# Attention scores in fp16 parts and packed banks: one change to a four-branch kernel on one Trainium2 core

## What is computed

```python
q, k = rope(q), rope(k)            # 32 query heads, 8 key heads, width 16
scores = einsum("bhqd,bhkd->bhqk", q, k) / 4
masked = where(causal, scores, NEG)
chunk_max = masked.reshape(b, 32, s, s // 16, 16).max(-1)
top = top_k(chunk_max, 8)          # 8 chunks of 16 keys for each query
allowed = causal & (in_top | (k_pos < 128) | (k_pos > q_pos - 128))
attn = softmax(where(allowed, scores, NEG))
out = attn @ v
```

## Time and profile before

| | |
|---|---|
| median of three runs | 1491.49 us |
| the profiled execution | 1492.17 us, of which the traced span is 1490.4 us |
| busy in the span: PE / DVE / ACT / POOL | 1314.6 / 1047.9 / 870.6 / 452.0 us |
| `project` | 472.8 to 602.9 us from the span's start |
| `attention` | 602.9 to about 1345 us |
| granted clock, mean | 0.938 |

### The profile page before, as it was taken

How to read it: one execution, slowest core, us unless ns; L and a number is a source line. 1 busy time by engine, 2 the same in 40 slices (tenths; PEclk the granted TensorE clock), 3 DMA queues, 4 the chain that set the end, 5 groups by cost and what they waited for, 6 DMA issues and landing times. The chain is left out here.

```text
span 1490.4 us, 35636 instructions
## 1 busy us (share of the span) xinstructions
PE 1314.6 (88%) x10686; PEld 697.9 (47%) x10686; DVE 1047.9 (70%) x3535; ACT 870.6 (58%) x1605; POOL 452.0 (30%) x1388
## 2 busy tenths in 40 slices
PE   8957999999996995799899898998989989986996
PEld 3423444444443553355455454554545545543663
DVE  5875656566553697688788787887878878852563
ACT  2525626354241564477678676776768767772553
POOL 3430000000002332344343343433433434431665
PEclk9976999999998997699999999999999999998997
DMA  9310000000000366301111011110111100002221
GB/s 339 144 42 1 1 1 0 0 0 0 0 1 4 102 161 160 129 5 36 41 39 39 7 36 41 39 39 7 39 37 39 39 13 33 10 9 57 57 78 43
DMA packets 65132, 69.74 MB, mean 47 GB/s; under 512 B 35214, under 2 KB 53774, under 8 KB 64300
## 3 DMA queue, kind: packets, MB, share of 16 engines
q1 hardware_dynamic: 64940, 67.38, 14.0%
HBM read 36.96 MB, written 19.92 MB: 38 GB/s over the span
## 5 line engine op out<-in xcount | busy, mean ns | idle before, releaser
L1362 DVE TENSOR_REDUCE arena<-bank 128x32 f32<-128x512 f32 (+3 forms) x768 | 395.7, 549 | 108.6 <-PE bank L1209 53.7
L1300 ACT ACTIVATE arena<-bank 128x512 f32<-128x512 f32 x576 | 336.2, 611 | 178.2 <-PE bank L1220 103.7
L1206 PE MATMUL bank<-arena 96*128 96x512 bf16 (+3 forms) x768 | 248.6, 348 | 27.8 <-issue 20.5
L1220 PE MATMUL bank<-arena 123*128 123x512 bf16 x576 | 225.4, 397 | 8.9 <-ACT arena L1300 6.9
L1239 PE MATMUL bank<-arena 128*32 128x128 f32 x4608 | 171.0, 276 | 12.2 <-ACT arena L1300 12.2
L579 PE MATMUL bank<-arena 128*128 128x512 f16 (+1 forms) x704 | 171.0, 386 | 0.0
L1458 POOL TENSOR_SCALAR arena<-arena 128x128 bf16<-128x128 bf16 x384 | 143.9, 375 | 43.8 <-DVE arena L1408 19.7
L1446 POOL TENSOR_TENSOR arena<-arena 128x4 f32<-128x4 f32 x128 | 25.6, 200 | 379.8 <-DVEq L1380 379.8
L1239 PEld LDWEIGHTS bank<-arena 128*32 128x32 f32 x4608 | 119.5, 109 | 43.0 <-ACT arena L1300 24.7
L1206 PEld LDWEIGHTS bank<-arena 96*128 96x128 bf16 x768 | 72.1, 100 | 119.2 <-DVE arena L1362 54.5
L205 POOL TENSOR_TENSOR arena<-arena 128x1 f32<-128x1 f32 x32 | 7.6, 236 | 383.3 <-DVE arena L201 382.9
(11 more groups left out here) (182 smaller groups left out, 2257.4 us busy)
## 6 DMA issues: line engine op xcount, KB each, us to landing
arena<-qk_rows SPq DMA_DIRECT2D x16, 960.0 KB, 4.8
qk_rows<-arena SPq DMA_DIRECT2D x16, 768.0 KB, 4.1
arena<-arena SPq DMA_DIRECT2D x32, 256.0 KB, 2.6
arena<-in_x SPq DMA_DIRECT2D x4, 1024.0 KB, 12.3
out<-arena SPq DMA_DIRECT2D x16, 256.0 KB, 2.1
qk_rows<-arena SPq DMA_DIRECT2D x16, 192.0 KB, 4.6
arena<-in_down_qT SPq DMA_DIRECT2D x1, 2816.0 KB, 25.6
arena<-in_up_qT SPq DMA_DIRECT2D x1, 2752.0 KB, 18.1
```

The source lines that it names most:

```text
L1206: last = pe.matmul(bank[:, 0:k1 - k0], query_aug[st.slot][0:ROWS, h * P:(h + 1) * P], key_aug[st.p][0:ROWS, k0:k1], start=True, stop=not d ...
L1220: last = pe.matmul(bank[:, :], key_aug[st.p][0:KROWS, j * P:(j + 1) * P], query_aug[st.slot][0:KROWS, f * N:(f + 1) * N], start=True, stop ...
L1300: act.activation(probs[u % PROBS], back_bank[u % 2][:, :], ACT.Exp, scale=float(HD) ** -0.5).then_inc(probs_ready, 1)
L1362: dve.tensor_reduce(out=cm[:, h * 64 + k0 // CHUNK:h * 64 + k1 // CHUNK], in_=score_bank[bank_of_score(front, number)][:, 0:k1 - k0].rearr ...
```

## The change

q and k are split into two fp16 parts instead of three bf16 parts: three part products, 48 rows instead of 96. The mask rows move from PSUM and operand row 96 to row 64, the rows between (48 to 63) being zeroed once. Minus the maximum is one fp16 row instead of three bf16 ones. All mask rows of a head (49) are in one set, so each head's mask is turned once and `keep_q` copies once. Score banks are filled to 512 columns, with a head ending and the next beginning inside a bank: a step has `i + 1` banks instead of 4 or 8. For `i < 2` only the maximum of each head is taken. `schedule` assumes 0.65 us for each bank.

The diff, cut to its core ("..." where lines are left out):

```diff
-ROWS = 6 * HD
+TERMS = 3
+ROWS = TERMS * HD
+MASK_AT = 64
-MASK_ROWS = 3 * CPT + PARTS
-KROWS = ROWS + MASK_ROWS
+MASK_ROWS = (SEQ_TILES - 2) * CPT + 1
+KROWS = MASK_AT + MASK_ROWS
...
     # project, ScalarE and VectorE
-                act.activation(slots(q_rows[b])[:, :, 0:3, :], q_of(part[b][0], 3), ACT.Copy)...
+                act.activation(slots(q_rows[b])[:, :, 0:2, :], q_of(part[b][0], 2), ACT.Copy)...
-                    dve_seq.mark(dve.tensor_tensor(out=rotated[b], in0=rotated[b], in1=high, op=ALU.subtract))
-                    dve_seq.wait(dve)
-                    dve_seq.mark(dve.tensor_copy(mid, rotated[b]))
-                    dve_seq.wait(dve)
-                    dve_seq.mark(dve.tensor_tensor(out=low, in0=rotated[b], in1=mid, op=ALU.subtract))
+                    dve_seq.mark(dve.tensor_tensor(out=low, in0=rotated[b], in1=high, op=ALU.subtract))
...
-                    dve_seq.mark(dve.tensor_copy(kk[:, :, 0:4:3, :], k_of(high, 2)))
-                    dve_seq.mark(dve.tensor_copy(kk[:, :, 5:6, :], k_of(high, 1)))
-                    dve.tensor_copy(kk[:, :, 1:5:3, :], k_of(mid, 2))
-                    dve.tensor_copy(q[:, :, 3:5, :], q_of(mid, 2))
+                    dve.tensor_copy(kk[:, :, 0:3:2, :], k_of(high, 2))
...
+                dve.memset(m.key_aug[k][32:MASK_AT, :], 0.0)
...
     # attention, TensorE
+            pe.wait_ge(query_blank, 1)
-                    last = pe.transpose(turn_bf[0:ROWS, ...], staged[st.p][:, at:at + ROWS], m.ident_bf)
+                    last = pe.matmul(turn_bank[0:ROWS, ...], staged[st.p][:, at:at + ROWS], m.ident_half, ...)
-                    for f in range(1 + st.two):
-                        last = pe.transpose(turn_bf[ROWS:KROWS, ...], w[:, h, f, 0:MASK_ROWS], m.ident_bf)
+                    last = pe.matmul(turn_bank[MASK_AT:KROWS, ...], w[:, h, 0:MASK_ROWS], m.ident_half, ...)
+                for h, k0, k1 in pieces(st.i, number):
+                    at = h * (st.i + 1) * P + k0 - number * N
+                    diagonal = k1 == (st.i + 1) * P
+                    last = pe.matmul(bank[:, at:at + k1 - k0], query_aug[st.slot][0:ROWS, ...], key_aug[st.p][0:ROWS, k0:k1],
+                                     start=True, stop=not diagonal)
+                    if diagonal:
+                        last = pe.matmul(bank[:, at + k1 - k0 - P:at + k1 - k0], m.ident_bf, m.causal, start=False, stop=True)
                 last.then_inc(scored, 1)
...
     # attention, ScalarE
-                if st.two:
-                    act.activation(query_aug[st.slot][0:ROWS, N:2 * N], turn_bf[0:ROWS, 0:N], ACT.Copy)
-                n = (1 + st.two) * N
-                act.activation(query_aug[st.slot][ROWS:KROWS, 0:n], turn_bf[ROWS:KROWS, 0:n], ACT.Copy)...
+                act.activation(query_aug[st.slot][MASK_AT:KROWS, :], turn_bank[MASK_AT:KROWS, 0:N], ACT.Copy)...
...
     # attention, VectorE: 8 memsets of query_aug rows 32 to 63 at the start, then
+                def peak(number):
+                    per = GQ // (i + 1)
+                    dve.wait_ge(scored, ring_of_score(front, number) + 1)
+                    dve.tensor_reduce(out=tp...[:, number * per:(number + 1) * per, 0:1],
+                                      in_=score_bank[...][:, :].rearrange("p (h d) -> p h d", h=per), axis=AXX, op=ALU.max)...
+                for number in range(i + 1):
+                    reduce(number)
+                    for h in range(GQ):
+                        if last_bank(i, h) == number - 1:
+                            best(h)
...
     # attention, GpSimd: five small products and differences become
+                pool.tensor_tensor(out=w[:, :, MASK_ROWS - 1:MASK_ROWS], in0=tp[:, :, 0:1], in1=neg_one.unsqueeze(2),
+                                   op=ALU.mult).then_inc(minus_ready, 1)
...
     # schedule
-        scores = [("score", st, n) for st in front for n in range(GQ * halves[st.i])]
+        scores = [("score", st, m) for st in front for m in range(st.i + 1)]
...
-                at += 0.25 + min((st.i + 1) * P - half * 512, 512) / 1000
+                at += 0.65
```

More of the change, by code:

```diff
@@ L49 @@
 NEG = -float(2.0 ** 100)
+DROP = -60000.0
 TAKEN = 3e38
@@ L801, in project @@
     rotated = [take(QK) for _ in range(2)]
-    part = [[take(QK, BF16) for _ in range(PARTS)] for _ in range(2)]
-    q_rows, k_rows = [take(HEADS * ROWS, BF16) for _ in range(2)], [take(KV * ROWS, BF16) for _ in range(2)]
+    part = [[take(QK, F16) for _ in range(2)] for _ in range(2)]
+    q_rows, k_rows = [take(HEADS * ROWS, F16) for _ in range(2)], [take(KV * ROWS, F16) for _ in range(2)]
     key_rows = take(SEQ)
@@ L1169, in turn_q @@
                     at = st.i * ST_TILE + h * ROWS
-                    last = pe.transpose(turn_bf[0:ROWS, h * P:(h + 1) * P], staged[st.p][:, at:at + ROWS], m.ident_bf)
+                    last = pe.matmul(turn_bank[0:ROWS, h * P:(h + 1) * P], staged[st.p][:, at:at + ROWS], m.ident_half, start=True, stop=True)
                 last.then_inc(top_turned, 1)
@@ L1180, in turn_k @@
                     at = (half * 4 + c) * ST_TILE + GQ * ROWS
-                    last = pe.transpose(turn_bf[0:ROWS, c * P:(c + 1) * P], staged[p][:, at:at + ROWS], m.ident_bf)
+                    last = pe.matmul(turn_bank[0:ROWS, c * P:(c + 1) * P], staged[p][:, at:at + ROWS], m.ident_half, start=True, stop=True)
                 last.then_inc(top_turned, 1)
@@ L1198, in score @@
                 ring = ring_of_score(st, number)
-                h, half = divmod(number, halves[st.i])
-                k0, k1 = half * 512, min((st.i + 1) * P, (half + 1) * 512)
                 bank = score_bank[bank_of_score(st, number)]
-                diagonal = k1 == (st.i + 1) * P
-                if h == 0 and half == 0:
+                if number == 0:
                     pe.wait_ge(top_kept, st.g * TT + (3 + st.at))
                 pe.wait_ge(reduced, ring + 1)
[L1206 to L1209, removed]
+                for h, k0, k1 in pieces(st.i, number):
+                    at = h * (st.i + 1) * P + k0 - number * N
+                    diagonal = k1 == (st.i + 1) * P
+                    last = pe.matmul(bank[:, at:at + k1 - k0], query_aug[st.slot][0:ROWS, h * P:(h + 1) * P], key_aug[st.p][0:ROWS, k0:k1],
+                                     start=True, stop=not diagonal)
+                    if diagonal:
+                        last = pe.matmul(bank[:, at + k1 - k0 - P:at + k1 - k0], m.ident_bf, m.causal, start=False, stop=True)
                 last.then_inc(scored, 1)
@@ L1217, in masked_score @@
                 pe.wait_ge(probs_ready, st.g * BK + (u + 1))
-                f = int(st.two and j >= 4)
                 extra = j == st.i or (j == st.i - 1 and st.i >= 2)
-                last = pe.matmul(bank[:, :], key_aug[st.p][0:KROWS, j * P:(j + 1) * P], query_aug[st.slot][0:KROWS, f * N:(f + 1) * N],
+                last = pe.matmul(bank[:, :], key_aug[st.p][0:KROWS, j * P:(j + 1) * P], query_aug[st.slot][0:KROWS, :],
                                  start=True, stop=not extra)
@@ L1326, in _ @@
         def _(dve):
+            for slot in range(SEQ_TILES):
+                last = dve.memset(query_aug[slot][32:MASK_AT, :], 0.0)
+            last.then_inc(query_blank, 1)
             dve.sem_inc(reduced, 3)
```

142 lines of the change are left out of this document (63 added, 79 removed).

## The result

The changed kernel takes 1588.89 us (median of four runs, 1587.06 to 1593.31), the kernel before on the same chip 1492.95: ratio 1.0638, 95% interval 1.0615 to 1.0661. The profiled execution took 1593.31 us, its span 1591.5. The forecast was 1546 within 1484 to 1610: slower, as said, but by 96 us and not by 55.

The account below looks back on a forecast made before the run. Three engines were near their limit, none at it; after the change TensorE's 94.6 us plus 5.3 of waits made turns of 99.9, 7.8 longer. Over 7.75 turns that is 60 us, less 5.5: 1546 us, range 1484 to 1610.

Parts of the forecast that it names:

- Shapes: TensorE in a loop turn: 204 more changes of operand shape at 0.094 us each, 19.2 us more.
- the term 25.2: TensorE's time for shape changes in a changed loop turn: 25.2 us, against 6.0 before.
- The rival of a free change: Into and out of each score: fewer rows cost no pause, or it is covered; 1443 us, chance 0.14.
- half price: Rival on TensorE's shape changes: 0.047 us each, about 1486 us, close to no change; chance 0.08.
- the whole drain: Rival: each shape change costs all the latency behind the stream, 0.167 us; about 1660 us, chance 0.02.
- Columns, waits: Loop turn on TensorE: 1.7 us fewer columns; bank waits (5.8) and turned-q waits (3.8) go, exponential waits (5.3) stay.
- The waits stay: Rival: TensorE still meets banks not ready, a turn 17.4 us longer; 1620 us, chance 0.06.
- 3.4 us at the turn's end: End of each loop turn: TensorE stands 3.4 us for nothing the profile shows, counted the same before and after.
- a clock below 0.96: Sign of being wrong: a granted clock under 0.96 in the attention stage, a cause not counted; no size given.
- were TensorE free: VectorE in a loop turn: 4 to 7 us less work, costed at nothing because TensorE is late.
- Project and start: End of project and start of attention: together 5.5 us saved, within 3 to 8.
- The eight memsets: Ahead of the first turn_k: TensorE's added wait for VectorE costs nothing, or about 2 us once without cover.

Follow-up runs that it names:

- experiment 1: Changed kernel with one zero row added, so the scores contract 65 rows instead of 48, the rest of the change kept: 1466.38 us, 0.982 of the kernel before.
- experiment 2: Kernel before with the chunk-choosing scores contracting 64 of their 96 rows, nothing else changed: 1570.84 us, ratio 1.0517.
- the slope: Written-out changed kernel with 65-row scores only in steps of i 2 or less, or 4 or more: 1508.24 and 1470.62 us, 0.087 and 0.098 us a change.
- written-out kernels: Changed kernel and kernel before, each with the attention stage's hardware loop written out as straight code: 1538.59 and 1462.46 us.
- experiment 3: Changed kernel with 65-row scores, and turned q and turned masks widened to 96 and 114 stationary columns: 1453.96 us, 0.9725 of the kernel before.

## Why the prediction was right, and what it missed

*Shapes.* Right, and in place and size: 0.107 us between stream and next start where 0.094 was taken, 0.09 to 0.10 as a slope. That 48 rows and 48 or 49 columns are shapes of their own, on which the 268 changes and so the term 25.2 rest, was the author's assumption, and an array's shape as such no run shows; the runs showed pauses of 0.097 to 0.109 us on the way into and out of just those operands, between groups that change 268 times a turn. Matmuls do run side by side at weighing, four of 128 columns starting 0.007 us apart and the next four 0.11 to 0.13 us after the first (kernel before, from 744.784); ahead of a score of the kernel after, none of 687 gaps behind another operand was below 0.097. The row nearest in kind (a 128x32 stretch) priced a shape that no row showed. Where only the columns of the shape change, the pause is still 0.097 (experiment 1, median of 64). The rival of a free change fell by experiments 1 and 2; half price by the slope; the whole drain by the 0.107 us, where it asked for 0.167.

*Columns, waits.* The forecast turn without its end is 99.9 - 3.4 = 96.5 us; written out it measures 97.26. So price, columns and remaining waits together are 0.8 us off, and that they come so close is luck in part. Which waits stay was turned round: the exponential's, said to stay whole, nearly went at the masked scores (TensorE now comes later to them), and the reductions', said to go, kept 3.3 us a turn; the two errors cancel. Nor does it prove much that 14.9 us of waits were left over and the table gave 15.0. Weighing's weight loads waited for exponentials as well, 13.9 us in five turns before (10.4 after), and were left out of the 15.0; and the 14.9 held the half clock behind the jump, 5.0 - 3.4 = 1.6 us a turn. "The waits stay" fell as a rival, for most of the 14.9 went.

*The step that failed* is the term "3.4 us at the turn's end", taken unchanged from before. The stall is unchanged, but what follows is not: 12.2 us at 1.2 GHz instead of 5.8. In them TensorE changes shape 17 times and stands 0.36 us: 12.2 - 17 x 0.107 - 0.4 = 10.0 us of streaming, half of it lost, 5.0 us, as the two stretches above show; with the stall 8.3. That is 4.9 a turn above the term, and with the 0.8 it is the whole miss of a loop turn, 105.6 against 99.9.

The total is not that miss times 7.75, for the loop jumps only six times. It adds up so: without jumps a turn grew by 97.26 - 87.1 = 10.2 us where 7.8 was forecast, 2.4 x 7.75 = 18 us; a jump grew by 8.3 - 5.0 = 3.3 where nothing was forecast, 6 x 3.3 = 20; the start of the stage gained 7.1 instead of 5.5, which takes 1.6 back. Together these are some 36.5 of the 41 us by which the loss exceeds the forecast. The 2.4 come from the 0.8 and from the 1.6 us of half clock, which the forecast carried in every turn of the kernel before and which a turn without its jump does not have. About 4 us are left over, and between the written-out kernels too (10.2 x 7.75 - 7.1 = 72 of the 76 measured), so they do not lie at the jumps; the longer half clock at the start of the stage, 38 us instead of 21.5, is the likely place, but no run isolates it.

The text had named a clock below 0.96 as the cause it had not counted; the sum should have priced that stretch, for the kernel before shows it too. That 1589 lies within the range at all is owed to the room left for waits, which went, and not to any room for the clock.

*VectorE.* Costed at nothing, as the gain "were TensorE free": experiment 1 has 356 us of VectorE in five turns where before had 376, 4 us a turn, the low end of the 4 to 7.

*Project and start.* From the end of the last product to the first reduction 20.3 us (581.78 + 1.89 to 603.95), where it was 27.4 (576.65 + 1.89 to 605.90): 7.1 less, forecast 5.5 within 3 to 8. The loop itself stayed with TensorE. The eight memsets cost nothing, as forecast: TensorE's first matmul waited for the load. Experiment 1, with 16 of them, starts 2.4 us later: 22.7 from last product to first reduction.

## What to carry to other kernels

When an edit narrows a stationary operand, look in its trace for a pause between it and its neighbours (here 0.105 to 0.109 us into and out of 48 and 64 rows, 0.006 with 65), and then count such changes in the order in which TensorE runs, not matmuls or columns. Where a narrow matmul alternates with full ones, a row of zeros that takes the pause away can be worth more than the rows saved: here it turned 6.4% slower into 1.8% faster, and with the turns widened and the loop written out into 5.7% faster (1407.34 us, ratio 0.9433, 0.9404 to 0.9463). A stall at a loop's jump is to be priced with the clock that follows it: here 3.1 to 3.4 us of stall, and 5.1 us (1.7 in the kernel before) of half clock.

## What was not expected of the hardware

The stretch at 1.2 GHz behind the same stall of 3.0 to 3.7 us is not a constant: 5.8 us of work before, 12.2 after, 8 to 11 with the narrow scores of experiment 2, where nothing but the scores' shape (and its pauses) was altered. At the start of the stage experiment 2 has 38.6 us of it, where the kernel before has 21.5. The pauses are not all of it: experiment 3 has fewer changes of shape than the kernel before. Its granted clock in two turns of the same instructions, from 817.00 and from 1082.80, where TensorE starts again at 817.15 and 1082.87:

```profile
817.00:822.00 5.00, 4.85 (x19) 2.60 (x20) 3.39 (x6) 2.75 (x7) 0.00 (x0) 0.50 0.02 5
822.00:827.00 5.00, 4.78 (x39) 2.81 (x39) 1.79 (x6) 2.61 (x5) 0.00 (x0) 0.53 0.02 5
```
```profile
1082.80:1087.80 5.00, 4.93 (x20) 2.65 (x21) 3.46 (x7) 2.83 (x7) 0.00 (x0) 0.50 0.02 5
1087.80:1092.80 5.00, 4.94 (x59) 3.04 (x62) 2.81 (x10) 3.16 (x7) 0.21 (x1) 0.82 0.02 5
```

By the same reading as above the first lasts until 826.7, the second until 1089.6: 9.6 and 6.7 us. What ends the stretch is left open; no run isolated it.
